# Transposed attention scores from plain keys and queries kept by head, in matmuls of 256 moving columns, and maxima added for two pairs of batches at once

## What is computed

```python
# L0: self attention (sa), strided cross attention (ca), feed-forward (f), each with a layer norm
scores = einsum('bhtd,bhsd->bhts', q, k) * SCALE          # sa: q, k, v from x;  ca: k, v from ctx
x = _ln(x + softmax(scores) @ v @ out_w.T + out_b)          # ca: only keys s with (s - h) % 4 == 0
x = _ln(x + gelu(x @ w1.T + b1) @ w2.T + b2)
# L1 (l1): cross attention with a key mask, then an update of the state and a layer norm
# L2 (l2, g): causal cross attention, layer norm, feed-forward
# L3 (l3): squared-relu attention on keys within 1 of an index
w = where(mask, square(relu(scores)), 0);  out = w / max(w.sum(-1), EPS_DEN) @ v
return x_tokens + out @ Wo.T
```

## Time and profile before

| | us |
|---|---|
| median of 3 runs | 292.65 (289.53 to 295.85) |
| profiled execution, its own time | 291.29 |
| its span, first to last instruction | 289.50 |
| PE busy (6903 matmul records) | 224.9 |
| PEld busy | 179.8 |
| DVE busy | 115.1 |
| ACT busy | 111.3 |
| POOL busy | 33.9 |

### The profile page before, as it was taken

How to read it: one execution, slowest core, us unless ns; L and a number is a source line. 1 busy time by engine, 2 the same in 40 slices (tenths; PEclk the granted TensorE clock), 3 DMA queues, 4 the chain that set the end, 5 groups by cost and what they waited for, 6 DMA issues and landing times.

```text
span 289.5 us, 14864 instructions
## 1 busy us (share of the span) xinstructions
PE 224.9 (78%) x6903; PEld 179.8 (62%) x6903; DVE 115.1 (40%) x215; ACT 111.3 (38%) x290; POOL 33.9 (12%) x63
## 2 busy tenths in 40 slices
PE   1797674699889799987969677697598787669583
PEld 0566653597568587776757466566476576557472
DVE  1598874055474301678714303123105013415041
ACT  0246122303635655338432331323154286425311
POOL 6920200001302113010101001011010100100000
PEclk9999997558999999999987957969979799999855
DMA  6930000000000000000000000000000000000000
GB/s 188 395 115 5 5 6 2 5 5 1 2 2 5 0 2 0 2 5 5 5 6 2 5 5 5 5 2 5 5 5 5 0 5 2 6 5 20 23 20 20
DMA packets 3773, 6.52 MB, mean 23 GB/s; under 512 B 512, under 2 KB 2944, under 8 KB 3456
## 3 DMA queue, kind: packets, MB, share of 16 engines
q1 hardware_dynamic: 3712, 5.57, 5.7%
HBM read 5.04 MB, written 0.52 MB: 19 GB/s over the span
## 4 chain that ended last, share of the span: by engine, by line
PE 66%; issue 16%; DVE 8%; ACT 7%; DMA 2%; SPq 1%; DVEq 0%; ACTq 0%
PE bank L431 30%; PE score L434 22%; PE bank L662 10%; DVE m_col_sb L913 6%; ACT probs_sb L766 3%; PE bank L637 3%; DMA xa_sb<-in_xT 2%; ACT hid_sb L814 1%; ACT att_sb L801 1%; DVE att_sb L940 1%; ACT xb_sb L806 1%; DVE rden_sb L938 0%; ACT attT_sb L797 0%; ACT L766 0%; ACT L814 0%
## 5 line engine op out<-in xcount | busy, mean ns | idle before, releaser
L434 PE MATMUL score<-q_kept_sb,k_kept_sb 32*64 32x64 f32 x2048 | 39.9, 249 | 14.7 <-issue 14.7
L766 ACT ACTIVATE probs_sb<-score 128x1024 f32<-128x1024 f32 (+1 forms) x28 | 26.3, 963 | 57.4 <-PE score L434 57.4
L913 DVE TENSOR_REDUCE m_col_sb<-score 128x32 f32<-128x2048 f32 (+1 forms) x16 | 30.2, 1890 | 39.6 <-PE score L434 39.6
L434 PEld LDWEIGHTS score<-q_kept_sb,k_kept_sb 32*64 32x64 f32 x2048 | 35.8, 141 | 16.3 <-issue 16.2
L431 PE MATMUL bank<-v_ext_sb,probs_sb 128*32 128x18 f32 (+1 forms) x2176 | 32.1, 200 | 16.8 <-issue 13.1
L431 PEld LDWEIGHTS bank<-v_ext_sb,probs_sb 128*32 128x32 f32 x2176 | 27.4, 124 | 26.5 <-issue 24.3
L434 PE MATMUL score<-m_row_sb,sel_sb 8*64 8x64 bf16 x768 | 26.8, 206 | 6.9 <-issue 4.8
L431 PE MATMUL bank<-xa_sb,W_sb 128*128 128x256 f32 x64 | 22.0, 468 | 8.2 <-DMA W_sb<-in_mats 4.3
L1030 POOL TENSOR_SCALAR vare_sb<-var_sb 128x2 f32<-128x2 f32 x20 | 4.5, 227 | 196.1 <-ACT att_sb L801 196.1
L434 PEld LDWEIGHTS score<-m_row_sb,sel_sb 8*64 8x64 bf16 x768 | 19.5, 110 | 8.5 <-issue 5.6
L975 DVE TENSOR_TENSOR att_sb<-bank,rstd_sb 128x256 f32<-128x256 f32 x20 | 8.4, 422 | 33.0 <-POOL rstd_sb L1032 33.0
(11 more groups left out here) (118 smaller groups left out, 379.0 us busy)
## 6 DMA issues: line engine op xcount, KB each, us to landing
W_sb<-in_mats SPq DMA_DIRECT2D x1, 1152.0 KB, 8.3
W_sb<-in_mats SPq DMA_DIRECT2D x1, 1024.0 KB, 10.5
ctxT_sb<-in_ctxT SPq DMA_DIRECT2D x1, 512.0 KB, 6.0
cn_sb<-in_ctx SPq DMA_DIRECT2D x1, 512.0 KB, 11.7
idx_sb<-in_idx SPq DMA_DIRECT2D x1, 512.0 KB, 6.7
out<-attT_sb SPq DMA_DIRECT2D x4, 128.0 KB, 1.9
xa_sb<-in_xT SPq DMA_DIRECT2D x1, 384.0 KB, 5.2
W_sb<-in_mats SPq DMA_DIRECT2D x1, 320.0 KB, 3.1
```

Source lines behind the costliest of these rows:

```text
L434: return pe.matmul(o, l, r, start=start, stop=True, skip_group_check=True)
L766: act.activation(dst, src, ACT.Exp, scale=SCALE).then_inc(sem("exp"), 1)
L913: dve.tensor_reduce(o, src, AX.X, ALU.max).then_inc(sem("max"), 1)
```

## The change

Three things change together.

- The transposed scores `t` now hold plain keys still (`k_kept`, 128 x 256, a copy by ScalarE with the bias) and move queries kept by head (`q_heads`, 128 x 4 x 256, written by VectorE from `q_kept`): 16 fp32 matmuls with 256 moving columns in place of 64 with 64. The step `s` still needs keys by head, now `k_heads`, which VectorE writes from the plain keys; l3, which has no `s`, has none. ca keeps its one masked copy.
- The negative maxima are added for both pairs `j` in one matmul of 2 x 64 columns: 32 in place of 64 (8 in place of 16 in ca). All masks come first, then the maxima, then the scores.
- To make room, values of l2 use the buffer of sa, values of l3 that of l1, the keys by head of l2 that of sa, and the index table lies in a part of the hidden buffer. The steps wait for the last reader (`V_BEFORE`, `k_free`). `timetable()` has the new steps `k_heads` and `q_heads` and makes a new order.

```diff
 KEYS = {"sa": 0, "l1": 1, "l2": 2, "l3": 0}
-VALUES = {"sa": 0, "ca": 1, "l1": 2, "l2": 3, "l3": 0}
-N_KEYS, N_VALUES = 3, 4
+VALUES = {"sa": 0, "ca": 1, "l1": 2, "l2": 0, "l3": 2}
+V_BEFORE = {"l2": "sa", "l3": "l1"}
+HEADS = {"sa": 0, "l1": 1, "l2": 0}
+N_KEYS, N_HEADS, N_VALUES = 3, 2, 3
...
             if name == "l3":
                 after = [("ctx_normed", "", g), ("gammas", "")]
-                k_free, v_free = [("t", "sa", g)], [("av", "sa", g, NJ - 1)]
-            k = add("pe", .6, "k", name, g, after=after)
-            add("dve", .45 if name == "ca" else 1.2, "k_kept", name, g, after=[k, load("small"), load("cols")] + k_free)
-            v = add("pe", .5, "v", name, g, after=after)
+                k_free, v_free = [("t", "sa", g)], [("av", "l1", g, NJ - 1)]
+            if name == "l2":
+                k_free, v_free = [("s", "sa", g)], [("av", "sa", g, NJ - 1)]
+            k = add("pe", .6, "k", name, g, after=after + k_free)
+            if name != "ca":
+                k = add("act", .42, "k_kept", name, g, after=[k, load("cols")] + k_free)
+            if name != "l3":
+                add("dve", .45 if name == "ca" else 1.25, "k_heads", name, g, after=[k, load("small"), load("cols")])
+            v = add("pe", .5, "v", name, g, after=after + v_free)
...
         def attention(name, k):
             k = add("pe", .6, "q", name, g, after=[k, load("w2" if name != "sa" else "w1")])
-            kept = add("act", .45, "q_kept", name, g, after=[k, load("cols")])
-            stacked = [kept, ("k_kept", name, g, 0)]
+            kept = [add("act", .42, "q_kept", name, g, after=[k, load("cols")])]
+            heads = [add("dve", 1.25, "q_heads", name, g, after=kept + [load("small")])] if name != "ca" else []
+            stacked = kept + [("k_heads", name, g, 0)] if name != "l3" else heads + [("k_kept", name, g, 0)]
...
-                stacked = [add("act", .4, "m_row", name, g, after=[k]), consts]
-            t = add("pe", {"ca": .5, "l1": 1.8, "l2": 2.}.get(name, 1.6), "t", name, g, after=stacked)
+                stacked = [add("act", .4, "m_row", name, g, after=[k]), consts] + heads
+                if name != "ca":
+                    stacked.append(("k_kept", name, g, 0))
+            t = add("pe", {"ca": .5, "l1": 1.9, "l2": 2.1}.get(name, 1.7), "t", name, g, after=stacked)
...
         q_kept = sb("q_kept", [128, G, GT])
-        k_kept = [sb(f"k_kept{i}", [128, G, HH, GT]) for i in range(N_KEYS)]
+        q_heads = sb("q_heads", [128, G, HH, GT])
+        k_kept = [sb(f"k_kept{i}", [128, G, GT]) for i in range(N_KEYS)]
+        k_heads = [sb(f"k_heads{i}", [128, G, HH, GT]) for i in range(N_HEADS)]
...
-        idx = sb("idx", [128, TOK], mybir.dt.int32)
+        idx = hid[:, 2, :].bitcast(mybir.dt.int32)
...
                                 if n == masks:
-                                    last = mm_onto(o, q_kept[rows_of(r), g, b * T:(b + 1) * T],
-                                                   key_columns(name, g, b, r), start=not masks)
+                                    k = (kc_kept[rows_of(r), g, of_batch(b)] if name == "ca"
+                                         else k_heads[HEADS[name]][rows_of(r), g, :, of_batch(b)])
+                                    last = mm_onto(o, q_kept[rows_of(r), g, of_batch(b)], k, start=not masks)
                                     continue
...
+                if name != "ca":
+                    pe.wait_ge(sem("q_heads"), nth("q_heads", name, g))
+                    pe.wait_ge(sem("k_kept"), nth("k_kept", name, g))
...
-                for j in range(NJ):
-                    def place(x, r):
-                        c = 64 * ((r + x) % 2)
-                        return score[c:c + 64, 2 * x + r // 2, j * GT:(j + 1) * GT].rearrange("p (h q) -> p h q", h=HH)
-
-                    for n in range(masks):
+
+                def place(x, r):
+                    c = 64 * ((r + x) % 2)
+                    return score[c:c + 64, 2 * x + r // 2, :].rearrange("p (j h q) -> p j h q", j=NJ, h=HH)
+
+                for n in range(masks):
+                    for j in range(NJ):
                         for x, r in tiles:
                             t = (g * GB + 2 * j + x) * T
                             if name == "l1":
...
-                            mm_onto(place(x, r), stat, mov, start=n == 0)
+                            mm_onto(place(x, r)[:, j, :, :], stat, mov, start=n == 0 and j == 0)
+                if name != "l3":
                     for h in range(1 if name == "ca" else HH):
-                        if name != "l3":
-                            for x, r in tiles:
-                                q = (2 * j + x) * T
-                                stat = (sel_ca[rows_of(r, 8), :, :].rearrange("p k h -> p (k h)") if name == "ca"
-                                        else sel[rows_of(r, 8), h, :])
-                                mm_onto(place(x, r)[:, h, :], stat, m_row[rows_of(r, 8), g, q:q + T], start=not masks)
                         for x, r in tiles:
-                            b = 2 * j + x
-                            k = key_columns(name, g, b, r)
-                            last = mm_onto(place(x, r)[:, h, :], k if name == "ca" else k[:, h, :],
-                                           q_kept[rows_of(r), g, b * T:(b + 1) * T], start=False)
+                            stat = (sel_ca[rows_of(r, 8), :, :].rearrange("p k h -> p (k h)") if name == "ca"
+                                    else sel[rows_of(r, 8), h, :])
+                            m = m_row[rows_of(r, 8), g, :].rearrange("p (j x q) -> p j x q", j=NJ, x=2)[:, :, x, :]
+                            mm_onto(place(x, r)[:, :, h, :], stat, m, start=not masks and h == 0)
+                for j in range(NJ):
+                    for x, r in tiles:
+                        b = 2 * j + x
+                        if name == "ca":
+                            last = mm_onto(place(x, r)[:, j, 0, :], kc_kept[rows_of(r), g, of_batch(b)],
+                                           q_kept[rows_of(r), g, of_batch(b)], start=False)
+                        else:
+                            last = mm_onto(place(x, r)[:, j, :, :], k_kept[KEYS[name]][rows_of(r), g, of_batch(b)],
+                                           q_heads[rows_of(r), g, :, of_batch(b)], start=False)
                 last.then_inc(sem("t"), 1)
...
+                elif step == "k_kept":
+                    act.wait_ge(sem("k"), nth("k", name, g))
+                    dst = k_kept[KEYS[name]][:, g, :]
+                    if name == "l3":
+                        act.wait_ge(sem("t"), nth("t", "sa", g))
+                        last = act.activation(dst, bank[g][:, 0:GT], ACT.Copy)
+                    else:
+                        last = act.activation(dst, bank[g][:, 0:GT], ACT.Identity, bias=col(f"{name}_kb"), scale=1.0)
+                    last.then_inc(sem("k_kept"), 1)
...
-                k = bank[g][:, 0:GT].unsqueeze(1).to_broadcast([128, HH, GT])
-                mask = const("head").unsqueeze(2).to_broadcast([128, HH, GT])
-                o = k_kept[KEYS[name]][:, g, :, :]
-                if name == "l3":
-                    dve.wait_ge(sem("t"), nth("t", "sa", g))
-                    last = dve.tensor_tensor(o, k, mask, ALU.mult)
-                else:
-                    last = dve.scalar_tensor_tensor(o, k, col(f"{name}_kb"), mask, ALU.add, ALU.mult)
-                last.then_inc(sem("k_kept"), 1)
+                if name == "l2":
+                    dve.wait_ge(sem("s"), nth("s", "sa", g))
+                dve.wait_ge(sem("k_kept"), nth("k_kept", name, g))
+                dve.tensor_tensor(k_heads[HEADS[name]][:, g, :, :],
+                                  k_kept[KEYS[name]][:, g, :].unsqueeze(1).to_broadcast([128, HH, GT]),
+                                  const("head").unsqueeze(2).to_broadcast([128, HH, GT]), ALU.mult
+                                  ).then_inc(sem("k_heads"), 1)
+
+            def queries_by_head(name, g):
+
+                dve.wait_ge(sem("q_kept"), nth("q_kept", name, g))
+                dve.wait_ge(sem("small_loaded"), 16)
+                last = dve.tensor_tensor(q_heads[:, g, :, :], q_kept[:, g, :].unsqueeze(1).to_broadcast([128, HH, GT]),
+                                         const("head").unsqueeze(2).to_broadcast([128, HH, GT]), ALU.mult)
+                last.then_inc(sem("q_heads"), 1)
```

44 lines of the change are left out of this document (22 added, 22 removed).

## The result

The changed kernel takes 246.51 us (median of 4 runs, 243.14 to 248.27), the kernel before 293.06 on the same chips (4 runs, 289.53 to 295.85): a ratio of 0.838, 95% interval 0.820 to 0.856. The forecast was 262, the range 246 to 281; by the ratio the time is 245.5, just under its lower end. The profiled execution took 243.14 us, so the drop to explain is 291.29 - 243.14 = 48.2 us, where the prediction had 29.5.

What follows compares the result with a forecast made beforehand. TensorE was taken to bound every stage, idling in issue gaps (41.6 us) read as late instruction supply. 291.3 - 10.5 (step t) - 24 (supply) + 5 (added work) = 261.8, forecast 262 us; range 246 to 281 us, 8 in 10.

Steps and rivals of the forecast that it cites:

- A: TensorE's step t: fewer, merged matmuls make t 1.5 us in place of 2.25, l3's part 1.12; -10.5 us.
- B: TensorE's instruction supply: fewer records leave issue gaps only in dense places, 17.6 us of 41.6; -24 us.
- The 3.8 us: TensorE's instruction supply: taken as the least time in which 127 matmuls can be supplied, 30 ns each.
- C: Added q_heads on VectorE and key copies on ScalarE, mostly beside TensorE; the uncovered part costs +5 us, from 0 to 20.
- Rival 2: VectorE is late and every q_heads is on the path: +20 us, time 277; chance 0.14.
- rival 4: q_heads waiting in VectorE's in-order queue holds up max_parts, 2.6 us each: slower than before, up to 298; chance 0.04.
- rival 3: Instruction supply stops binding nearly everywhere: gaps give -38 us, added work +3, time 246; chance 0.14.
- the four parts below 286.8: Outcomes counted as faster, 0.89 in sum: the forecast's own case (0.58), rivals 2 and 3, half of rival 1.
- Rival 1: Gaps on TensorE are cover: with supply on time it waits for maxima or exponentials instead; time 286, chance 0.10.

Runs made afterwards that it cites:

- e5: Kernel before plus 64 useless fp32 matmuls of 224 columns, two behind each half av; 309.9 us, ratio 1.067.
- e1: Changed kernel with both the score and the maxima matmuls of t cut back into the old pieces; 299.6 us, 1.028 of the kernel before.
- e9: Changed kernel with each of its sixteen q_heads operations written twice; 253.0 us, 0.868 of the kernel before.
- e14: Changed kernel plus 768 useless one-column bf16 matmuls, 48 ahead of each hidden-layer matmul of the first feed-forward layer; 264.9 us, 0.920 of the kernel before.
- e2: Changed kernel with only its keys-against-queries matmuls of t cut back to 64 columns; 284.9 us, 0.979 of the kernel before.
- e3: Changed kernel with only its maxima matmuls cut back to 64 columns; 261.2 us, 0.893 of the kernel before.
- e8: Changed kernel with av in matmuls of 64 queries, two tiles side by side, in place of 32 in four; median 261.7 us, executions 247.7 to 270.3.
- e15: Kernel before with attention weights and values in bf16, one record for an av matmul in place of two; 278.5 us, ratio 0.960.
- e18: Changed kernel plus 768 useless bf16 matmuls in the first feed-forward layer, each moving 64 columns; 265.9 us, 0.903 of the kernel before.
- e4: Kernel before with only the maxima merged for two pairs and the masks first; 288.0 us, ratio 0.989.
- e6: Changed kernel plus 64 useless fp32 matmuls of 224 columns, two behind each half av; 256.7 us, 0.882 of the kernel before.

## Why the prediction was right or wrong

**A, -10.5: right.** A `t` takes 1.45 us where 1.5 was said, and 1.09 in l3 where 1.12 was, at full clock and without a gap. By the rule of the Trainium skill, "TensorE: Matmul & The Clock Gate", section "Back-to-back issue gap", the sum was estimated at 280. The measured `t` contradicts it, as the earlier trace rows did.

**B, -24: right.** Issue went from 41.6 to 16.9 us, -24.7; packets and records are as said. e5 shows the mechanism by itself, a block of 127 records that lasts 3.93 us with twice the work in it. The 3.8 us are a mean of the earlier trace rows and not "the least time": one block there took 3.45. "Mostly hidden", as the Trainium skill has it in "Runtime: NRT & Kernel Launch", section "Instruction fetch mechanics", does not hold for this kernel.

**C, +5: right in size, as far as it can be told.** TensorE's idle time other than issue rose by 1.6 us (64.6 - 41.6 = 23.0 before, 41.5 - 16.9 = 24.6 after); e1 gives +7.7 for everything that is not merging, of which 5.3 is busy time that goes with its lower clock; e9 gives +6.5 to +8.8 for doubling `q_heads`. Rival 2 (+20) and rival 4 are out. The chain shows VectorE most in the first attention.

**What failed: the sum held no term for the granted clock.** The prediction read 0.81, 0.87 and 0.84 in the stages with gaps and 1.00 without, and wrote of it only, in rival 3, that "the granted clock would help", at 0.14. With A and B as measured and C between 1.6 and 7.7, the profiled time would be 258 to 264; it was 243. What is missing is in TensorE's busy time. The span fell by 49.2 us (1.1 us more than before lies outside it): 26.1 of busy time, of which 10.5 is A, and 23.1 of idle time, which is the 24.7 of issue less the 1.6 of other waits. The 15.6 us of busy time that are left are just under the 16.9 at which the fall of half clock from 68.3 to 26.9 us was estimated. The views were there: 68.3 us at half clock with 55.0 us of work in it puts up to 27 us at stake, and the bound of that term belonged in the range. Rival 3 had the time (246) for a wrong reason: it had B at -38. A slip beside it: the four parts below 286.8 add to 0.91, not 0.89.

**Rival 1, gaps as cover: hardly, in the long stage.** Maxima and exponentials are 18.1% of its chain, but of a shorter stage: 16.3 us of 90.3, where they had 17.8 of 118.7. Only the 4.2 us of `rstd` are new among the leading entries. In the first attention it holds in part: VectorE's leading entries grew from 5.6 to 14.7 us of the chain.

**Shown and argued.** That the merging gives all of the gain is shown (e1), and so is that the clock costs dear matmuls their time (e14: 1.22 against 0.70 us). That the clock rose in the changed kernel is read from its profile; that the 15.6 us come from it is argued from that estimate, and no run holds the clock fixed. Why it rose is not settled: half clock falls from 94 to 27 us along e1, e2, e3 and after, together with the gaps; e8 and e14 have it with few gaps, with small or cheap matmuls; e15 has fewer records and no less half clock; e18, which has the gaps of e14 and moves 64 columns in each pad in place of one, has 10.2 us of it in that stage in place of 23.9, in one execution each.

## What to carry to other kernels

Cut TensorE's list into stretches of equal instruction count: where they all last nearly the same (here 3.45 to 4.12 us for some 127 matmuls), the array's work in them is free and each record removed pays, here 25 ns for one of the scores and 35 for one of the maxima, the clock's part included. Give the granted clock a term of its own, from zero to half of the busy time that lies at half clock, and put both ends into the range; it can also go the other way, as in e1 and e4. Merge matmuls only as far as the tiles side by side remain: half the records in half the tiles gained nothing in e8, one record in place of two through bf16 in `av` gave another 16 us.

## What was not expected of the hardware

- A `nop` that increments a semaphore costs some 150 ns of the kernel's time on TensorE: 2048 of them 316 us, 2040 of them 306, most of it at half clock.
- 48 bf16 matmuls with 128x32 weights and one column take 0.45 us, 9 ns each, at full and at half clock alike.
- With TensorE busy 90% of the time, its clock stayed at half for 23.9 us (e14).
- 1024 `av` records in two tiles are busy 44.1 us, 2048 in four tiles 26.1 (the first with 92 us of its kernel at half clock; at full clock half an `av` is 1.11 against 0.74 us).
- Most of one execution of e6 ran at a granted clock of 0.65: 312.6 us, where three others of the same kernel took 256.
